# Linear attention inside a two-layer block: scores made one chunk ahead, with a three-part ring for the masked scores and a transform moved between the chunks

## The reference

```python
def step(S, inp):                       # one chunk of 128 tokens
    qb, kb, vb = inp
    scores = einsum('bchd,bshd->bhcs', qb, kb) * D[None]       # decay mask
    o_intra = einsum('bhcs,bshd->bchd', scores, vb)
    o_inter = einsum('bchd,bhde->bche', qb, S) * q_decay
    S_new = chunk_decay * S + einsum('bshd,bshe->bhde', kb * k_decay, vb)
    return S_new, o_intra + o_inter
...
o = o * sigmoid(gate)                   # gate = x Wg1 Wg2
o = o * rsqrt(mean(o * o over a head) + eps) * norm_w
x = layernorm(x + o @ Wo)
```

## Time and profile before

| | us |
|---|---|
| median of three runs | 1914.0 (1907.09 to 1917.93) |
| the profiled execution | 1919.3 |
| its span, first to last instruction | 1917.4 |
| TensorE busy | 1769.0 (92%) |
| VectorE busy | 1334.2 (70%) |
| ScalarE busy | 983.7 (51%) |
| GpSimdE busy | 1277.3 (67%) |
| DMA | 427.32 MB, mean 223 GB/s |

### The profile page before, as it was taken

The page is one execution under the profiler, slowest core; times in us unless marked ns, Lnnn a source line. Parts: engine busy times, 40 slices in busy tenths (PEclk is TensorE's granted clock), DMA queues, the critical chain, the costliest instruction groups (busy, mean ns, idle before and its releaser), DMA issues. The chain is left out here.

```text
span 1917.4 us, 27445 instructions
## 1 busy us (share of the span) xinstructions
PE 1769.0 (92%) x9472; PEld 1159.1 (60%) x9472; DVE 1334.2 (70%) x1537; ACT 983.7 (51%) x1671; POOL 1277.3 (67%) x987
## 2 busy tenths in 40 slices
PE   7898998798998999989899899988999999999998
PEld 5566666476855665555555556554556556567886
DVE  2525334323248999799897999889999999994222
ACT  5344342566565656655666455555555655453212
POOL 4533542155539998688887989778989798893111
PEclk9999999899999999999999999999999999999999
DMA  7442332487758887678776887677778777775662
GB/s 241 130 141 73 122 117 69 157 293 278 264 187 288 290 297 257 217 253 284 233 248 230 280 278 252 235 235 235 240 254 290 239 255 265 272 259 163 204 193 99
DMA packets 159226, 427.32 MB, mean 223 GB/s; under 512 B 30992, under 2 KB 54096, under 8 KB 158704
## 3 DMA queue, kind: packets, MB, share of 16 engines
q1 hardware_dynamic: 159088, 425.57, 66.0%
HBM read 356.30 MB, written 69.21 MB: 222 GB/s over the span
## 5 line engine op out<-in xcount | busy, mean ns | idle before, releaser
L1563 ACT ACTIVATE decay<-delta_on_states,a_neg 128x512 f32<-128x512 f32 x512 | 352.2, 692 | 249.6 <-DVE h_states L1720 232.6
L1819 POOL TENSOR_TENSOR q_or_raw_or_h_times_c<-h_states,c_rep 128x512 f32<-128x512 f32 x293 | 381.8, 1316 | 71.7 <-PE scan_y L1397 41.4
L1819 POOL TENSOR_TENSOR h_times_c_rest<-h_states,c_rep 128x512 f32<-128x512 f32 x219 | 283.9, 1307 | 45.2 <-DVE h_states L1720 22.1
L1785 POOL TENSOR_TENSOR h_lo<-silu_in_h_lo,h_hi 128x512 fp32r<-128x512 f32 x128 | 168.3, 1315 | 207.7 <-ACT h_hi L1470 197.2
L1720 DVE TENSOR_TENSOR_SCAN h_states<-decay,h_last,d_b 128x512 f32<-128x512 f32 x192 | 242.7, 1277 | 9.6 <-ACT decay L1563 5.4
L84 PE MATMUL gate<-x_hi,w 128*128 128x512 f32 x512 | 233.6, 456 | 11.6 <-DVE silu_in_h_lo L1646 6.4
L1720 DVE TENSOR_TENSOR_SCAN h_states<-decay,d_b 128x512 f32<-128x512 f32 x192 | 231.2, 1215 | 15.8 <-ACT decay L1563 11.7
L84 PE MATMUL up<-x_hi,w 128*128 128x512 f32 x512 | 231.1, 451 | 2.3 <-DVE silu_in_h_lo L1652 2.3
L84 PE MATMUL y_or_aux<-h_hi,w 128*128 128x512 f32 x468 | 207.0, 442 | 7.5 <-DVE x L1658 4.0
L1388 PE MATMUL du_spread<-stack,selectors 96*128 96x512 bf16 x512 | 157.8, 390 | 58.0 <-DVE d_b L1697 38.0
L85 PE MATMUL gate<-x_lo,w 128*128 128x512 f32 x512 | 203.5, 397 | 0.0
(11 more groups left out here) (226 smaller groups left out, 3448.6 us busy)
## 6 DMA issues: line engine op xcount, KB each, us to landing
w<-w_split SPq DMA_DIRECT2D x336, 512.0 KB, 3.8
delta_on_states<-delta SPq DMA_DIRECT2D x256, 512.0 KB, 5.4
w_split<-w_presplit_hi_lo SPq DMA_DIRECT2D x32, 512.0 KB, 3.5
w_split<-w SPq DMA_DIRECT2D x16, 1024.0 KB, 7.2
w_presplit_hi_lo<-in_w13b SPq DMA_DIRECT2D x32, 256.0 KB, 3.6
q_or_raw_or_h_times_c<-in_w13a SPq DMA_DIRECT2D x16, 512.0 KB, 4.5
w_split<-w_presplit SPq DMA_DIRECT2D x16, 512.0 KB, 5.6
delta_x_parts<-delta_x_parts_out SPq DMA_DIRECT2D x16, 384.0 KB, 4.6
```

The source lines that it names most:

```text
L1563: act.activation(da[:, s % ND], dring[:, s % NR], ACT.Exp, scale=a[:, column(s):column(s) + 1]).then_inc(s_da, 1)
L1785: pool.tensor_tensor(hl[:, idx % RH], sg[:, idx % RH], hh[:, idx % RH].bitcast(F32), ALU.subtract).then_inc(s_hl, 1)
L1819: pool.tensor_tensor(hc[s % NC_], hs[:, s % NH], crep[:, tile_of(s // SPO) % 2], ALU.mult).then_inc(s_hc, 1)
```

## The change

- The masked scores get a ring of three halves, `probs[:, 0:3]`, each for two of the four j. Chunk n uses halves 2n and 2n + 1, modulo 3. The four parts that were `pr` are the first two halves; the tile `part` moves into the third.
- TensorE makes the scores of the next chunk ahead of the other products of this one, and the product with the masked scores stands before the state's update.
- VectorE masks chunk c + 1 before it gates and updates the state for chunk c. Its third mask of a chunk waits for the previous chunk's `from_chunk`, whose half it overwrites.
- The two halves of the second transform go from their place ahead of `kT` to places behind the chunks 1 and 2. The lists of the PSUM order follow; ScalarE's, GpSimdE's and SyncE's orders are not edited.
- k's decay is kept for 16 heads instead of 512 columns and read through a broadcast; its own load is gone.

```diff
-        kdec = p.sb("k_decay", [P, D])
+        kdec = p.sb("k_decay", [P, NH])
...
-        pr = p.sb("probs", [P, HPT, KD, CH])
-        part = p.sb("partial_sums", [P, TT])
+        probs = p.sb("probs", [P, 3, HPT // 2, KD, CH])
+        pr = probs[:, 0:2].rearrange("p h a b c -> p (h a) b c")
+        part = probs[:, 2, 0].rearrange("p b c -> p (b c)")
...
+        def probs_of_heads(n, j):
+            return probs[:, (2 * n + j // 2) % 3, j % 2]
...
         NEXT = (["mp"] + ["q"] * 2 + ["mb"] + ["q"] * 2 + ["had0"] * 2 + ["vp"] + ["norm"] * KD + ["vb"] + ["k"] * KD
-                + ["v"] * CPT + ["gate"] * KD + ["had1"] * 2 + ["kT"] * CPT + ["wo"] * KD)
+                + ["v"] * CPT + ["gate"] * KD + ["kT"] * CPT + ["wo"] * KD + ["had1"] * 2)
...
-                sp.dma_start(kdec[:, :], ld_cols).then_inc(s_kd, 16)
...
-                    def transform(i):
-
-                        pe.wait_ge(s_bf, BF * (2 * t + i) + BF)
-                        for half in range(2):
-                            out = bank(f"had{i}", half)
-                            rows = had[0][:, half * (NC // 2):(half + 1) * (NC // 2), :]
-                            pe.matmul(out, const[:, C_HAD:C_HAD + P],
-                                      rows.rearrange("p c d -> p (c d)")).then_inc(s_pj, 1)
+                    def transform(i, half):
+                        if half == 0:
+                            pe.wait_ge(s_bf, BF * (2 * t + i) + BF)
+                        out = bank(f"had{i}", half)
+                        rows = had[0][:, half * (NC // 2):(half + 1) * (NC // 2), :]
+                        pe.matmul(out, const[:, C_HAD:C_HAD + P],
+                                  rows.rearrange("p c d -> p (c d)")).then_inc(s_pj, 1)
...
-                    transform(1)
                     for c in range(CPT):
                         out = bank("kT", c)
...
                     scores_of(0)
                     for c in range(CPT):
-                        from_state(c)
-                        state_update(c)
-                        from_chunk(c)
                         if c + 1 < CPT:
                             scores_of(c + 1)
+                        from_state(c)
+                        from_chunk(c)
+                        state_update(c)
+                        if c in (1, 2):
+                            transform(1, c - 1)
...
-                    act.wait_ge(s_kd, 16)
-                    act.activation(kdec[:, :], kdec[:, :], ACT.Exp,
+                    act.activation(kdec[:, :], ldt, ACT.Exp,
                                    scale=early[:, E_REV:E_REV + 1]).then_inc(s_dexp, 1)
...
-                        dve.tensor_tensor(kd[:, c, :], rd.bank("kT", c), kdec[:, :], ALU.mult)\
-                           .then_inc(s_dt, 1)
+                        dve.tensor_tensor(kd[:, c, :].rearrange("p (h e) -> p h e", h=NH),
+                                          rd.bank("kT", c).rearrange("p (h e) -> p h e", h=NH),
+                                          kdec[:, :].unsqueeze(2).to_broadcast([P, NH, HD]), ALU.mult).then_inc(s_dt, 1)
...
-                    for c in range(CPT):
+                    def probs_of(c):
                         n = CPT * t + c
                         for j in range(HPT):
                             dve.wait_ge(s_sc, HPT * n + j + 1)
-                            dve.tensor_tensor(pr[:, j], scores[:, j], dmask[:, j], ALU.mult).then_inc(s_pr, 1)
-
+                            if c and j == HPT // 2:
+                                dve.wait_ge(s_o, n)
+                            dve.tensor_tensor(probs_of_heads(n, j), scores[:, j], dmask[:, j], ALU.mult).then_inc(s_pr, 1)
+
+                    probs_of(0)
+                    for c in range(CPT):
+                        n = CPT * t + c
+                        if c + 1 < CPT:
+                            probs_of(c + 1)
+                        dve.wait_ge(s_o, n + 1)
+                        gated = sig[:, :, c * CH:(c + 1) * CH]
+                        dve.scalar_tensor_tensor(out=gated, in0=gated, scalar=1.0, in1=o_ps[:, :, :],
+                                                 op0=ALU.add, op1=ALU.mult).then_inc(s_og, 1)
                         dve.wait_ge(s_u, n + 1)
                         for m in range(KD):
                             mm = dve.scalar_tensor_tensor(out=st[:, m], in0=st[:, m], scalar=cdec[:, m:m + 1],
                                                           in1=u_ps[:, m], op0=ALU.mult, op1=ALU.add)
                         mm.then_inc(s_st, 1)
-                        dve.wait_ge(s_o, n + 1)
-                        gated = sig[:, :, c * CH:(c + 1) * CH]
-                        dve.scalar_tensor_tensor(out=gated, in0=gated, scalar=1.0, in1=o_ps[:, :, :],
-                                                 op0=ALU.add, op1=ALU.mult).then_inc(s_og, 1)
                         dve.wait_ge(s_st, n + t + 2)
```

More of the change, by code:

```diff
@@ L86, in three_passes, with attention_phase @@
     return pe.matmul(out, w_lo, x_hi, start=False, stop=last)
-def attention_phase(nc, x, qT, w13a, s_raw13, en, cn, w13b, w13x, x_dram, aw_d, ld_tok, ld_feat, ld_cols, wg1_d, wg2_d, nw_d, w2n, w2h):
+def attention_phase(nc, x, qT, w13a, s_raw13, en, cn, w13b, w13x, x_dram, aw_d, ld_tok, ld_feat, wg1_d, wg2_d, nw_d, w2n, w2h):
     with ExitStack() as ctx:
@@ L151, in attention_phase @@
         s_bh, s_bo = p.sem("attn_presplit_hi"), p.sem("attn_presplit_lo")
-        s_zero, s_kd = p.sem("attn_cleared"), p.sem("k_decay_in")
+        s_zero = p.sem("attn_cleared")
         s_lc, s_lq, s_lr, s_ln = (p.sem(f"attn_norm_{n}") for n in ("centred", "squares", "rstd", "x"))
@@ L164, in by_piece @@
             return (whole, count) if k == KD - 1 else (piece, k + 1)
-        FIRST = (["q"] * KD + ["had0"] * 2 + ["k"] * KD + ["v"] * CPT + ["gate"] * KD + ["had1"] * 2
-                 + ["kT"] * CPT)
+        FIRST = (["q"] * KD + ["had0"] * 2 + ["k"] * KD + ["v"] * CPT + ["gate"] * KD
+                 + ["kT"] * CPT + ["had1"] * 2)
         SECOND = (["q"] * KD + ["had0"] * 2 + ["norm"] * KD + ["k"] * KD + ["v"] * CPT + ["gate"] * KD
-                  + ["had1"] * 2 + ["kT"] * CPT + ["wo"] * KD)
+                  + ["kT"] * CPT + ["wo"] * KD + ["had1"] * 2)
         NEXT = (["mp"] + ["q"] * 2 + ["mb"] + ["q"] * 2 + ["had0"] * 2 + ["vp"] + ["norm"] * KD + ["vb"] + ["k"] * KD
-                + ["v"] * CPT + ["gate"] * KD + ["had1"] * 2 + ["kT"] * CPT + ["wo"] * KD)
+                + ["v"] * CPT + ["gate"] * KD + ["kT"] * CPT + ["wo"] * KD + ["had1"] * 2)
         TAIL = ["norm"] * KD + ["wo"] * KD
@@ L425, in from_chunk @@
                                 hs = slice((m * HPT + j) * HD, (m * HPT + j + 1) * HD)
-                                mm = pe.matmul(o_ps[j * HD:(j + 1) * HD, m, :], v[:, c, hs], pr[:, j, m, :],
+                                mm = pe.matmul(o_ps[j * HD:(j + 1) * HD, m, :], v[:, c, hs], probs_of_heads(CPT * t + c, j)[:, m, :],
                                                start=False, stop=True, skip_group_check=True, tile_position=(0, j * HD))
@@ L445, in body @@
                         pe.wait_ge(s_const, 16)
-                    transform(0)
+                    transform(0, 0)
+                    transform(0, 1)
                     if rd.norms_x:
@@ L1846, in _, with program @@
                         pre_low(PRE_AT[tick - 4])
-def program(nc, x_d, en, cn, w2n, aw, ld_tok, ld_feat, ld_cols, wg1_d, wg2_d, nw_d, w13a, sel_d, ysel_d, bsel_d,
+def program(nc, x_d, en, cn, w2n, aw, ld_tok, ld_feat, wg1_d, wg2_d, nw_d, w13a, sel_d, ysel_d, bsel_d,
             wall_d, wdt_d, fp_d, al_d, w13b, w2b, out):
@@ L1857, in program @@
         s_raw13 = [p.sem(f"raw13_in{b}") for b in range(2)]
-        attention_phase(nc, x, first, w13a, s_raw13, en, cn, w13b, w13x, x_d, aw, ld_tok, ld_feat, ld_cols, wg1_d, wg2_d, nw_d, w2n, w2h)
+        attention_phase(nc, x, first, w13a, s_raw13, en, cn, w13b, w13x, x_d, aw, ld_tok, ld_feat, wg1_d, wg2_d, nw_d, w2n, w2h)
         trunk_phase(nc, x, first, s_raw13, w13a, w2h, w13x, w2b, sel_d, ysel_d, bsel_d, wall_d, wdt_d, fp_d, al_d, out)
@@ L1915 @@
         "ld_feat": np.ascontiguousarray(np.repeat(ld, HD).reshape(KD, P).T),
-        "ld_cols": np.ascontiguousarray(np.broadcast_to(np.repeat(ld, HD), (P, D))),
         "wg1": rows(n["L0_attn_Wg1"]),
```

## The result

The changed kernel takes 1970.6 us (median of 5 runs, 1968.39 to 1976.92) against 1914.0 before (1907.09 to 1917.93): slower, ratio 1.0294 with a 95% interval of 1.0275 to 1.0313, or 56.6 us on the medians. The forecast was 1960, with a range of 1943 to 1973.

What follows compares the result with a forecast made beforehand. TensorE, busy 314 of attention's 363 us, was taken to bound the kernel. -0.5 - 1.8 - 1.2 + 14.0 + 12.2 + 12.2 + 9.3 + 1.8 = +46.0 us gave 1960 on the median, range 1943 to 1973.

Steps and rivals of the forecast that it cites:

- the loop: Attention's chunk loop: the wait for masks is replaced by waits for state and ring, 4.74 us a chunk against 4.81.
- The 2.3 us of order per round: Chunk loop: the new order alone makes it 2.3 us longer per round, counted inside the late blocks.
- The late block: ScalarE's and GpSimdE's in-order work behind the second transform makes the next first transforms 14.0, 12.2 and 12.2 us late.
- the block: From ScalarE's take of the last transformed half, 17.9 us after the round's first scores, to the last butterfly: 26.7 us.
- rival (c): Round transitions: butterflies come in time and TensorE's own path decides, 10.0 us each; +37.6, 1952 us; 17 in 100.
- the fall behind the waits ahead of q: Three round transitions: half clock after stalls of 5.5 to 6.5 us loses about 2.5, covered by GpSimdE's block.
- the sum: All terms of the forecast, from the start to the tail: +46.0 us; this forecast was given 63 in 100.
- Rival (d): Behind the late transform: half clock is not covered, 2.5 us more at each of three transitions; +53.5, 1967; 15 in 100.
- 0.4 gained in each of rounds 1 to 3: Transposes without the second transform ahead of them: 0.4 us gained a round, 1.2 in all, as VectorE holds the third.
- The tail: Round 3 into the tail: ScalarE's squares of the outputs come 9.3 us late, behind its high parts.
- The 1.8 for norm products at half clock: Tail: the four norm products go at half the clock between ScalarE's steps, 1.8 us late by the last.
- 6.6 of slack: Round 0 of the kernel before: the block's last butterfly ended 6.6 us before the next first transform began.

Runs made afterwards that it cites:

- x5: Changed kernel with a ring of four halves instead of three; decay masks of j = 2, 3 share those of j = 0, 1: 1960.7 us, ratio 1.0238.
- x1: Changed kernel with the second transform back in its old place ahead of the transposes: 1936.5 us, ratio 1.0095 to the kernel before.
- x2: Kernel before with only the second transform's halves moved behind the scores that follow chunks 1 and 2: 1960.5 us, ratio 1.0229.
- x3: Changed kernel with ScalarE's high parts and x cast, and SyncE's stores and loads of these blocks, ahead of their waits for the second transform: 1937.7 us, ratio 1.0104.
- x4: Changed kernel with VectorE's product of q and its decay waiting for the first slice's last butterfly in rounds 1 to 3: 1968.5 us, ratio 1.0264.
- x6: x1 with from_state(0) made ahead of scores(1) in the first chunk of each round: 1925.8 us, ratio 1.0060 to the kernel before.
- x7: x1 with VectorE's masks in two pairs around the gate and TensorE's order scores, from_chunk, state_update, from_state: 1907.0 us, ratio 0.9955 to the kernel before.
- x8: x7's loop with the second transform behind chunks 0 and 1 and ScalarE's and SyncE's orders of x3: 1916.9 us, ratio 1.0011 to the kernel before.

## Why the prediction was right, and where it was off

**What bounds it, the loop.** Right. The distance was forecast at 4.74 and is 4.80 between the last scores of a round; masks wait for the ring, from_state for the state (x5 takes the ring's wait away and the state's wait falls to 0.5). The 2.3 us of order per round show in x1.

**The late block.** Right, and shown twice: made alone in x2 (+44 us), and taken away alone in x3 (-33). The take was forecast at S + 17.9, the block at 26.7 us, the transforms 14.0, 12.2 and 12.2 late; measured are S + 19.4 to 20.6, 26.0 to 28.0, and 16.9, 13.3 and 14.2. TensorE waited for GpSimdE at all three (4.4, 1.3 and 1.7 us), so rival (c) fell. Without the slow butterfly the block took 26.0 or 26.1 in each: 0.6 or 0.7 less than in round 0 of before, most of it between the low parts of x and the first butterfly (5.6 to 5.7 us against 6.2), where ScalarE waits for the loads.

**The clock.** This is the term that was mis-sized. I priced the fall behind the waits ahead of q, and there it was covered, as forecast (half clock from 88 to 93, the transform still waits 4.4 for a butterfly). (The prediction puts TensorE at that transform by 43.5; its own terms, 40.6 + 2.5, give 43.1, and nothing hangs on the difference.) I did not price the loop's own waits: 2.66 us in chunk 0 of every round, with half the clock behind it each time. They put the take of the last half 1.5, 1.7, 2.7 and 1.7 later, 7.6 us in sum, of the 9.2 that the sum was short. That it is the clock and not the order shows in x1, where the same loop reaches its third scores at S + 8.5 with the clock whole and at S + 9.9 to 10.1 without. Rival (d) was right in one of its three transitions: behind the late transform of round 1 the clock was at half from 107 to 110, and TensorE came 1.4 us later to the transposes than before (35.4 us after T1 instead of 34.1). In the other two, where the transform had waited 1.3 and 1.7, the clock stayed whole, and so it did in x4, where the transform of round 1 waited 1.8. So the measured 1970.6, which is nearer to rival (d)'s 1967 than to my 1960, is not its case.

**The transposes.** The step "0.4 gained in each of rounds 1 to 3" failed. VectorE did start on them 0.1 after its low parts, but TensorE, without the transform to do, stood 2.98 us for it instead of 1.4, and then ran some 4 us of the output product at half clock. From T to S the three rounds are +1.4, +0.6 and +1.0 instead of -0.4 each, 4.3 in sum; 1.4 of this is the slow start behind the late transform just named, 2.9 is here. The table has the us from the start of the transposes, or of the transform where it stands ahead of them, to S:

| | clock whole | clock fell |
|---|---|---|
| transform in its old place (before, x1, x6, x7) | 17.6 to 17.8, 7 rounds | 18.8 to 18.9, 5 rounds |
| transform moved (after, x2 to x5, x8) | none | 18.4 to 19.8, 18 rounds |

The clock can fall here in both orders, and in the kernel before it did in round 1. With the transform moved it fell in all 18 rounds, and what the empty place might gain shows in none.

**GpSimdE's last butterfly** took 2.0 longer in round 1, which was in no term. The Trainium skill (SBUF — State Buffer, section "SBUF: two separate sides") says that a VectorE operation with two SBUF inputs and a GpSimdE one that reads SBUF exclude each other for a whole instruction. The trace agrees: 3.31 against 1.29 us beside such a product, 1.26 when x4 moves it away. The trace of the kernel before had shown this price, ahead of the first loop:

```profile
41.55 2.29 DVE L698 TENSOR_TENSOR attn_w_lo<-probs,attn_w_hi 128x2048 fp32r<-128x2048 f32 x1 [8.79 <-ACT attn_w_hi L494]
...
41.56 3.43 POOL L665 TENSOR_TENSOR had_a<-had_b 128x512 f32<-128x512 f32 x1
```

**The tail.** Squares 10.8 late against 9.3 (the loop's clock again). The 1.8 for norm products at half clock didn't come: they did run at half clock (0.50 from 393 to 397), but the output product began 11.15 us after the squares, as before (11.14). That product itself was 0.9 quicker, as the half clock ended earlier in it.

Against the terms: 7.6 (loop's clock) + 1.4 (half clock behind the late transform) + 2.9 (transposes) + 2.0 (butterfly) - 2.7 (tail) - 1.9 (faster loads and rounding) = 9.3, and the sum was short by 9.2. Of the 13.9 us that were missing, 11.9 lie where the clock fell and the sum had no half clock.

## What to carry to other kernels

When work moves later on one engine, follow every in-order queue behind its consumer into the next iteration and subtract its slack: here 20.6 us later less 6.6 of slack gave a forecast of 14, and 16.9 came. A wait that a new order brings into a loop can cost a second time, by half clock behind it: mostly 1.4 to 1.6 us for a wait of 2.7 us here. A prefetch into a single set of banks wins nothing if the freed wait comes back as a ring or state wait; write the closed loop of the new order down, step by step, before building it, and use the same sum to look for the order that is shorter (x7: split the masks around the gate). A place that looks like a cost may be filling a wait that remains.

## What the runs showed of the hardware

- TensorE's clock fell to half behind waits that I had taken as short. Behind 2.65 or 2.66 us for the masks it fell in all 16 rounds of the changed kernel, x3, x4 and x5 (0.50 granted from 63 to 66 in the first), and in two of the four rounds of x1. Behind 2.4 us for the state it fell in all four rounds of x1 and in two of the four of x6. Behind the waits of 1.2 to 1.65 us in the loops it never did. But a wait of 1.4 us and the transposes behind it, in the kernel before, x1, x6 and x7, were followed by half clock in 5 of 12 rounds, so the length of the wait alone doesn't decide.
- A fall in the loop cost 1.4 to 1.6 us (2.6 in round 2 of the changed kernel), one behind the transposes 1.1 to 1.2 where the transform kept its place.
- VectorE's q product and its 128-column AND went from 2.29 and 0.28 us to 2.50 and 1.35 beside a butterfly, and the butterfly from 1.29 to 3.31. In rounds 2 and 3, where the butterfly had begun first, only VectorE's product grew, to 2.75 and 3.16.
